# Pivot row and pivot column of a reflection computed in two parts

## The reference

```python
deg = jnp.sum(A, axis=0) + jnp.sum(A, axis=1) - jnp.diagonal(A)
L_norm = d_inv_sqrt[:, None] * (jnp.diag(deg) - A) * d_inv_sqrt[None, :]
_, U = jnp.linalg.eigh(L_norm)
agg = jnp.einsum('mn,bnd->bmd', U.T, features)
h = jax.nn.relu(agg @ W1 + b1)
out = jnp.einsum('nm,bmd->bnd', U, h @ W2 + b2)
```

## Time and profile before

| what | value |
|---|---|
| median of 3 runs | 4364.65 us |
| profiled execution, its span | 4359.52 us, 4357.7 us |
| TensorE matmul busy | 2952.5 us, 68% |
| VectorE busy | 2978.4 us, 68% |
| ScalarE busy | 982.9 us, 23% |
| GpSimd busy | 764.9 us, 18% |
| the chain that ended last, by engine | VectorE 42%, TensorE 39%, issue 7%, ScalarE 6%, GpSimd 5% |
| mean granted TensorE clock | 0.818 of full speed |

### The profile page before, as it was taken

The page is one execution under the profiler, slowest core; times in us unless marked ns, Lnnn a source line. Parts: engine busy times, 40 slices in busy tenths (PEclk is TensorE's granted clock), DMA queues, the critical chain, the costliest instruction groups (busy, mean ns, idle before and its releaser), DMA issues.

```text
span 4357.7 us, 70705 instructions
## 1 busy us (share of the span) xinstructions
PE 2952.5 (68%) x21286; PEld 1968.4 (45%) x21286; DVE 2978.4 (68%) x18190; ACT 982.9 (23%) x3671; POOL 764.9 (18%) x3343
## 2 busy tenths in 40 slices
PE   2899998888888899999710011010064958699998
PEld 1677777777777765555410000000042623354433
DVE  6677888888888868888878889999822122414323
ACT  0222222322322212222210000000013121336532
POOL 0121222222222222333222221111000000000000
PEclk6789999999989959999855555555587979799998
DMA  2000000000000000000000000000000000000000
GB/s 97 2 2 2 2 2 2 2 2 2 2 2 2 2 1 2 2 2 2 1 0 0 0 0 0 0 0 0 0 0 0 0 19 0 0 0 0 1 0 39
DMA packets 3104, 21.16 MB, mean 5 GB/s; under 512 B 432, under 2 KB 560, under 8 KB 1072
## 3 DMA queue, kind: packets, MB, share of 16 engines
q1 hardware_dynamic: 2736, 16.85, 1.0%
HBM read 12.66 MB, written 4.19 MB: 4 GB/s over the span
## 4 chain that ended last, share of the span: by engine, by line
DVE 42%; PE 39%; issue 7%; ACT 6%; POOL 5%; DMA 0%; DVEq 0%; POOLq 0%; ACTq 0%; SPq 0%
PE ps L1023 6%; DVE H L1895 6%; PE ps L710 4%; DVE jq L1469 3%; PE ps L718 3%; POOL step L1077 3%; PE ps L1030 2%; DVE H L1469 2%; POOL C L1078 2%; ACT sz L1290 2%; DVE PQ L1647 2%; PE ps L566 2%; PE ps L660 2%; PE ps L945 2%; DVE SO L1676 1%
## 5 line engine op out<-in xcount | busy, mean ns | idle before, releaser
L718 PE MATMUL ps<-C 128*32 128x131 f32 (+39 forms) x10200 | 379.4, 279 | 16.6 <-DVE C L1664 15.1
L710 PE MATMUL ps<-eye,same 128*128 128x384 f32 x766 | 365.9, 562 | 0.0
L1077 POOL TENSOR_SCALAR step<-XYEG,PQ 128x8 f32<-128x8 f32 (+3 forms) x510 | 158.6, 311 | 1147.7 <-DVE PQ L1647 1147.7
L1290 ACT ACTIVATE sz<-C,PQ 128x4 f32<-128x4 f32 (+3 forms) x510 | 151.6, 297 | 785.0 <-POOL C L1078 785.0
L1023 PE MATMUL ps<-C,V 128*128 128x512 f32 (+1 forms) x504 | 285.9, 724 | 8.4 <-issue 8.4
L718 PEld LDWEIGHTS ps<-C 128*32 128x32 f32 x10200 | 256.6, 115 | 54.5 <-DVE C L1664 20.6
L1274 ACT ACTIVATE tsc<-tsc 128x1 f32<-128x1 f32 x510 | 103.5, 203 | 726.6 <-DVE tsc L1608 726.6
L1469 DVE CUSTOM_DVE_ANT_0 jq<-SO,ps,C 128x10 f32<-128x10 f32 (+14 forms) x1199 | 220.6, 229 | 64.6 <-PE ps L740 12.1
L727 PEld LDWEIGHTS ps<-dots,C 128*128 128x128 f32 x1020 | 172.7, 201 | 182.1 <-DVE dots L1469 94.2
L740 PE MATMUL ps<-C,XYEG 128*128 128x2 f32 (+1 forms) x958 | 186.4, 270 | 101.3 <-POOL C L1078 98.8
L1895 DVE RECIPROCAL H<-H 128x8 f32<-128x8 f32 (+8 forms) x81 | 242.3, 2992 | 2.8
(11 more groups left out here) (515 smaller groups left out, 7414.6 us busy)
## 6 DMA issues: line engine op xcount, KB each, us to landing
out_x<-X SPq DMA_DIRECT2D x4, 1024.0 KB, 3.9
X<-in_x SPq DMA_DIRECT2D x2, 1280.0 KB, 20.3
X<-in_x SPq DMA_DIRECT2D x1, 1536.0 KB, 16.6
eye<-in_eye SPq DMA_DIRECT2D x1, 1026.0 KB, 9.0
WK<-in_adj SPq DMA_DIRECT2D x1, 1024.0 KB, 5.0
adjT<-in_adjT SPq DMA_DIRECT2D x1, 1024.0 KB, 7.0
WK<-in_below SPq DMA_DIRECT2D x1, 1024.0 KB, 11.0
V<-in_wih SPq DMA_DIRECT2D x1, 1024.0 KB, 4.8
```

The costliest lines, as they stand in the source:

```text
L710: mm(ps[:, 7, 0:n], ident, eye[:, 0, 0:n], start=True, stop=True)
L718: m = mm(ps[q * QUAD:(q + 1) * QUAD, 0, 0:c + n], SI[:, b, 0, 2 * j:2 * j + 1].broadcast_to([P, QUAD]), AS[:, b, q, k * QUAD:P + n], start ...
L1077: step(g_.tensor_scalar(step2[:, k:KB, :], this[:, :, 2:4], PQ[:, r % 2, 1:2], None, ALU.mult))
L1290: fn(sz[:, k:KB].unsqueeze(2), SI[:, k:KB, 0, 2 * j + 1:2 * j + 2], ACT.Copy, scale=PQ[:, r % 2, 2:3])
```

## The change

A reflection is "parted" if it is not the first of its panel, r > 1, and its block is one of the first three (nb > 1). That holds for 359 of the 510. For a parted reflection r + 1:

- pivot_row and its wait for zu_ready are gone from TensorE. In their place pivot_parts stands right behind L730: three matmuls (two where j = 1), one for the older pairs (2j - 2 columns), one for two numbers of x and y, one for a number of g. They need only e and the g of the reflection before. The wait for zu_ready moves to the row matmuls of the next reflection, which now wait for x_ready and zu_ready.
- On VectorE the newest pair's two numbers are made by two single-number operations (newest), the reductions over the older pairs (older_column, 2j - 2 columns) move ahead of the copy to drow and of the new column of SO, and two operations of 128 x nb elements add the newest pair behind it.

```diff
+def parted(r):
+    return r % PANEL > 0 and 1 < r < N - 1 and r // P < KB - 1
...
                 pe.wait_ge(S["x_ready"], r)
+                if parted(r):
+                    pe.wait_ge(S["zu_ready"], r - 1)
...
                 mm(ps[:, 1, 1:2], spread(XYEG[:, r % 2], k, 2), XYEG[:, r % 2, k, 3:4], start=True, stop=True).then_inc(S["pivot_ps"], 1)
+                if parted(r + 1):
+                    pivot_parts(r + 1)
                 pause(r, 1)
-                if (r + 1) % PANEL > 0 and r + 1 < N - 1:
+                if (r + 1) % PANEL > 0 and r + 1 < N - 1 and not parted(r + 1):
                     pivot_row(r + 1)
+
+            def pivot_parts(r):
+                k, j = r // P, r % PANEL
+                pe.wait_ge(S["e_ready"], r)
+                pe.wait_ge(S["g_ready"], r - 1)
+                if j > 1:
+                    mm(ps[:, 2, 0:2 * j - 2], spread(XYEG[:, r % 2], k, 2), SI[:, k, 0, 0:2 * j - 2], start=True, stop=True)
+                mm(ps[:, 2, NS:NS + 2], spread(XYEG[:, r % 2], k, 2), XYEG[:, (r + 1) % 2, k, 0:2], start=True, stop=True)
+                mm(ps[:, 2, NS + 2:NS + 3], spread(XYEG[:, r % 2], k, 2), XYEG[:, (r + 1) % 2, k, 3:4], start=True, stop=True).then_inc(S["g_ps"], 1)
...
+                split = not last and parted(r + 1)
                 ch.need(m_tz)
                 m_uz = ch.mark(stt(uz, tz, mu, uy, ALU.mult, ALU.add))
+                if split:
+                    dve.wait_ge(S["g_ps"], pivots(r + 1))
+                    go(ts_(newest[:, 1:2], ps[:, 2, NS + 2:NS + 3], mu, ps[:, 2, NS + 1:NS + 2], ALU.mult, ALU.subtract))
+                    m_new = ch.mark(ts_(newest[:, 0:1], ps[:, 2, NS:NS + 1], -1.0, None, ALU.mult))
                 ch.need(m_uz)
                 m_k2 = ch.mark(tt(k2, uz, ns2, ALU.mult))
+                if split:
+                    old = XYEG[:, (r + 1) % 2, k:KB, 3]
+                    if j > 0:
+                        m_old = older_column(r + 1)
+                    else:
+                        old = a_column(k, r + 1)
                 dve.wait_ge(S["scaled"], r)
                 go(v.tensor_copy(drow[:, r:r + 1], xy))
                 ch.need(m_k2)
                 stt(column(SO, k, 2 * j), x, k2, szv, ALU.mult, ALU.add).then_inc(S["so_done"], 1)
-                if not last and r + 1 < N - 1 and nb > 1:
+                if split:
+                    g = XYEG[:, (r + 1) % 2, k:KB, 3]
+                    ch.need(m_old if j > 0 else m_new)
+                    m_g = ch.mark(stt(g, column(SO, k, 2 * j + 1), newest[:, 1:2], old, ALU.mult, ALU.add))
+                    dve.wait_ge(S["so_done"], r)
+                    ch.need(m_g)
+                    stt(g, column(SO, k, 2 * j), newest[:, 0:1], g, ALU.mult, ALU.add).then_inc(S["g_ready"], 1)
+                elif not last and r + 1 < N - 1 and nb > 1:
                     pivot_column(r + 1)
```

More of the change, by code:

```diff
@@ L339, in build @@
         jk = sb("jk", [P, 2, KB])
+        newest = sb("newest", [P, 2])
         pick = sb("pick", [P, QUAD])
@@ L1676, in reflect, with older_column @@
                 stt(column(SO, k, 2 * j), x, k2, szv, ALU.mult, ALU.add).then_inc(S["so_done"], 1)
-                if not last and r + 1 < N - 1 and nb > 1:
-                    pivot_column(r + 1)
+                if split:
[6 more added lines that the diff above has]
+                elif not last and r + 1 < N - 1 and nb > 1:
+                    pivot_column(r + 1)
+            def older_column(r):
+                k, j = r // P, r % PANEL
+                a = AS[:, :, r % P // QUAD, r // P * QUAD + r % QUAD]
+                for b in range(k, KB):
+                    m = ch.mark(ttr(jq[:, b, 0:2 * j - 2], SO[:, b, 0:2 * j - 2], ps[:, 2, 0:2 * j - 2], XYEG[:, r % 2, b, 3:4], init=a[:, b:b + 1]))
+                return m
             def pivot_column(r, known=False):
```

## The result

The changed kernel takes 4490.8 us (median of 4 runs, 4474.38 to 4501.75) against 4364.12 us for the kernel before in the same comparison (4358.47 to 4366.91): ratio 1.0289, 95% interval 1.0255 to 1.0322. It is slower, as forecast, but by 127 us, not 50, and above the range. The profiled execution took 4474.38 us (span 4472.6) with a mean granted clock of 0.81, so the traces differ by 114.9 us. Matmul busy rose to 3161.6 us, VectorE busy to 3118.4 us.

The account below looks back on a forecast made before the run. No single engine bounds it; TensorE and VectorE wait for each other, VectorE ending second-block pair-late turns. Terms 13 + 5 - 3.5 + 15 + 14 + 6 = 50 us on 4364.65 gave 4415 us, range 4358 to 4452.

Parts of the forecast that it names:

- the 0.15 gained by L727: TensorE's row matmuls, pair late: could start 0.29 us after new x instead of 0.44, but VectorE hides the gain.
- the price of a turn with the clock-keeping matmul: After the Euler work, TensorE queues longer: 15 x 0.95 = 14 us at half clock, 28 x 0.23 = 6 at full.
- the two new numbers at 0.36 and 0.43: VectorE, second block: the two single-number operations start 0.36 and 0.43 us after the new x starts being made.
- the second, which needs the first's result, 0.25 later: VectorE's tail: second added operation starts 0.25 us behind the first, at 1.51, and L1608 at 1.64.
- pair late = 13 us: Turns waiting for GpSimd's pair, first three blocks: 80 x 0.01, 116 x 0.045 and 66 x 0.11 = 13 us lost.
- dots late: Turns where row matmuls waited for new x behind Euler pieces: 50 x 0.21 / 2 = 5 us lost.
- first turns: First turns of a panel (j = 1, 23 of them) lose their reductions: about -0.15 each, -3.5 us.
- single turns at half clock: 28 pivot rows loaded at half clock in the changed stretches: +0.55 us each on both engines, 15 us.
- Rival 2: TensorE decides, not VectorE: 120 turns gain up to 0.15 us, 4372 us, no change to speak of; chance 0.14.
- Rival 4: Wait for zu_ready only moves to the row matmuls: same 50 us cost, no TensorE gain; no chance given.
- rival 1: VectorE's tail hidden and the 83 us at half clock gone: 4352 us, faster; 0.15 with other ways to gain.
- Rival 3: Half clock lasts longer, through the 28 turns up to 1764 us: +60 us, 4475 us; chance 0.07.

Follow-up runs that it names:

- e3: Changed kernel with the two numbers written to PSUM, reductions over all columns back at their old place, no two added operations: 4384.76 us, ratio 1.0084.
- e14: e3 with the first new number as scalar_tensor_tensor and the two waits of the first reduction in the other order: 4354.52 us, ratio 1.0009.
- e2: Changed kernel with the first new number made by scalar_tensor_tensor instead of tensor_scalar with two pointer scalars: 4411.42 us, ratio 1.0127.
- e12: Changed kernel with the two waits of the last added operation in the other order: 4432.47 us, ratio 1.0193.
- e10: Kernel before with the two waits of the first reduction in the other order: 4332.34 us, ratio 0.9941.
- e7: Changed kernel with the split only up to r = 335, the code of before from there on: 4455.27 us, ratio 1.0244.
- e1: Kernel before with the three matmuls added behind L730, results unused, everything else as it was: 4485.48 us, ratio 1.0316.
- e4: Changed kernel with two matmuls instead of three, y and g in one and x's number left out: 4374.0 us, ratio 1.0052.
- e6: Changed kernel without the clock-keeping matmul behind the three new ones: 4495.32 us, ratio 1.0322.
- e5: Changed kernel with only the first of the three matmuls, both numbers read from it: 4369.58 us, ratio 1.0032.
- e8: Kernel before with VectorE's wait for the pivot row moved from the first reduction to the copy to drow: 4333.87 us, ratio 0.9947.
- e11: e8 with the two waits at the copy to drow in the other order: 4330.27 us, ratio 0.9953.

## Why the prediction was wrong

**Right: the direction and its mechanism.** VectorE's order ends the turn and the 0.15 gained by L727 stays off the path. L727 starts 0.28 to 0.29 after x in the first two blocks (forecast 0.29), though only at 0.33 in the third; the first new number starts at 0.36 to 0.37 (forecast 0.36), though at 0.44 in the third; the three matmuls stand 0.22 apart.

**Right in size: the price of a turn with the clock-keeping matmul.** Forecast +0.23 at full clock and +0.95 at half clock; measured +0.25 and +1.07. At half clock TensorE ends the turn, as forecast. At full clock the number is luck: I had the rows end the turn, 0.06 ahead of L1608, and they do so in e3 and e14 (+0.22 there), but in the changed kernel they are done at 1.53 and VectorE's longer order ends the turn at 1.70.

**Wrong, the first step: "the two new numbers at 0.36 and 0.43".** The second came at 0.57. I took the spacing of L1608 and L1610, 0.07, for an operation that takes two single numbers besides its input and lasts 0.28; it holds the next for 0.21. e2 takes 0.06 of these 0.14 back.

**Wrong, the second step: "the second, which needs the first's result, 0.25 later".** It was 0.32: the prediction saw that two waits can cost 0.11 (the 0.36 ahead of the first reduction) and still left it in the bounds instead of the sum. e12 and e10 show that it is the order of the two waits, 0.07 and 0.11.

These two moved the forecast end of the turn from 1.64 to 1.82 in the second block: +0.14, +0.07 and some hundredths less for the shorter reductions (0.15 instead of 0.16). Against the median of before (1.58, where I had taken 1.60 from one turn) that is +0.25 where I had 0.045. In the first block it is +0.30 where I had 0.01 to 0.03: the end came at 1.99 instead of 1.81, and before it had stood at 1.69 or less, not at 1.77 to 1.80. In the third it is +0.30 where I had 0.11. There my working has a slip too: one reduction less than 1.64 is 1.48, not 1.53, so the same count gives +0.06; the end came at 1.72, 0.07 of it because the first number came at 0.44. So "pair late = 13 us" is the term that failed. Whole turns from x to x, the same reflections at full clock in both traces, rose by 0.17, 0.21 and 0.25 us on the mean and by 0.22, 0.24 and 0.31 at the median (in the first block a part is hidden behind Euler pieces that end the turn anyway). Over 119, 119 and 74 turns that is 64 to 78 us, and with 45 turns x 0.25 = 11 behind them 75 to 89 of the 115 us. The terms for dots late (5), for first turns (-3.5) and for single turns at half clock (15) can't be told apart in these runs.

**Wrong, the third: that the half-clock stretches stay as they were.** The remaining 26 to 40 us (an estimate, by difference) go with more time at half clock: 317 us instead of 221 up to r = 335, and 106 instead of 79 from there to 382. That is 123 us more; a turn with the clock-keeping matmul took 5.09 instead of 3.48 us at half clock before, so about a third of such time is extra, some 40 us (also an estimate). I priced a turn at half clock but took the number of such turns from the trace of before. e7 and e1 show that it moves both ways: 0 us and some 230 us at half clock in the same 47 reflections. So a single repair is worth more than its share of the turn: by the ratios e2 took back 71 us, of which 20 are turns, e12 42, e4 103, and their sum, 216 us, is more than the whole loss. What decides when the clock falls or comes back stays open; no run here isolates it.

**The rivals.** Rival 2 (TensorE decides) is out: e3 and e14 keep its gain, and e14 is no faster than the kernel before. Rival 4 is out: in the second block L727 was held by L1099 once, for 0.2 us. Half of rival 1 is possible, since in e3, e4 and e7 the long half-clock stretch did not come back, but in the changed kernel r = 336 to 382 had 106 us at half clock, and the other half, a hidden tail, is not there. Rival 3 has nearly the measured number, 4475, by the wrong mechanism: half clock did reach the 28 turns behind (79 us of it), but the stretch ahead of them got shorter, and all of r = 336 to 382 gave 23 of the 115 us.

## What to carry to other kernels

Before moving an operation off one engine's path, find which engine ends the turn; if it is the other one, as here, the gain is void and the operations added there are paid. Price a new operation by a row of its own form (operands, single numbers, where it reads), not by the smallest spacing in sight, and where an operation waits for two semaphores, let it carry the one that comes last itself. Where the granted clock has two levels, a forecast needs a range for the time at the lower one, and an experiment must be judged by its turns at one level as well as by its total. Sums over stretches of one trace should not be read finer than two executions of the same code differ.

## What the runs showed of the hardware

- The same arithmetic on single numbers held the next VectorE operation for 0.21 us as tensor_scalar with two numbers from memory (0.28 long) and for 0.14 as scalar_tensor_tensor (0.22 long).
- With two waits, an operation started 0.11 (e10) and 0.07 us (e12) earlier when the semaphore that comes last was its own wait and not that of the separate instruction ahead of it.
- Three small matmuls a turn whose results no one reads cost nothing where TensorE had been waiting (blocks 2 and 3 of e1: 847 against 848 us), and 80 us in the two stretches behind, where the rows queue behind them and the granted clock was 0.58 and 0.59 against 0.53 and 1.00.
- With the same code up to r = 335, three traces (after, e6, e7) had 317, 322 and 366 us at half clock there; the stretch of r = 336 to 351 had between 0 (e4, e5, e7, e8, e11, e14) and 82 us (e1).
